# Graph attention and mixture of experts: groups 2 and 3 of the last stage treated as one unit

## The reference, cut to what matters

```python
def _gat_conv(x, W, att_src, att_dst, bias, src, dst):
    xw = (x @ W).reshape(N, H, CPH)
    e = leaky_relu(a_s[src] + a_d[dst], NEG)
    p = exp(e - segment_max(e, dst)[dst]);  alpha = p / segment_sum(p, dst)[dst]
    return segment_sum(xw[src] * alpha[:, :, None], dst).reshape(N, H * CPH) + bias
...
out = concatenate([h0, h1]) + x               # h0, h1: the two convolutions
x = x + layernorm(out) * gamma + beta
h = layernorm(x)                              # input of the experts
top_w, top_i = top_k(h @ Wg + bg, 2);  top_w = softmax(top_w)
out = x + sum over e of w_dense[:, e] * (gelu(h @ W1[e] + b1[e]) @ W2[e] + b2[e])
```

## Time and profile before

| | us |
|---|---|
| three runs, lowest, median, highest | 3035.05, 3036.59, 3038.42 |
| the profiled execution | 3036.07 |
| its span in the trace | 3034.2 |
| last stage, from the first `shares` to the first turned expert tile | 2007 to 2281 |
| busy in the whole span: PE, DVE, ACT, POOL | 2131.5, 2188.6, 1630.6, 1885.4 |

### The profile page before, as it was taken

One profiled execution on the slowest core, in us unless ns is written; L12 is line 12 of the kernel. 1 busy time (PEld: TensorE's weight loads), 2 busy tenths in 40 slices (PEclk: granted clock), 3 DMA queues, 4 the chain that ended last, 5 costly groups with the idle time before them and its releaser, 6 DMA issues.

```text
span 3034.2 us, 42972 instructions
## 1 busy us (share of the span) xinstructions
PE 2131.5 (70%) x11674; PEld 2015.1 (66%) x11675; DVE 2188.6 (72%) x4468; ACT 1630.6 (54%) x2613; POOL 1885.4 (62%) x1868
## 2 busy tenths in 40 slices
PE   4600002788887887888888888703449999999998
PEld 2400002787887787887878887603438999999997
DVE  7678877788887787888888887788864444444443
ACT  5424423687777776877777777624433333333332
POOL 5777767777777777777777777777771222222222
PEclk8855555898999898989998998855559999999999
DMA  9446993444444444444444444565772222222222
GB/s 357 135 145 179 159 239 123 127 127 143 147 128 127 140 150 127 127 152 139 128 127 147 143 127 127 167 218 168 260 257 37 38 37 37 38 38 37 38 37 31
DMA packets 278910, 395.04 MB, mean 130 GB/s; under 512 B 156236, under 2 KB 231569, under 8 KB 272257
## 3 DMA queue, kind: packets, MB, share of 16 engines
q1 hardware_dynamic: 202945, 244.92, 25.4%
q0 software_dynamic: 74000, 145.58, 20.9%
q10 hardware_dynamic: 1840, 3.06, 0.3%
HBM read 201.61 MB, written 191.79 MB: 130 GB/s over the span
## 4 chain that ended last, share of the span: by engine, by line
POOL 45%; PE 26%; issue 15%; DVE 7%; DMA 3%; ACT 2%; DVEq 2%; SPq 0%; POOLq 0%; ACTq 0%
POOL AR L935 43%; PE ps L1453 12%; PE ps L1459 12%; POOL placed L1003 1%; PE ps L1329 1%; DMA tables<-AR 1%; DVE group_stats L2020 1%; ACT AR L1262 1%; DVE AR L1718 1%; DVE AR L1765 1%; DMA state<-AR 1%; POOL AR L967 0%; DVEq L1760 0%; POOL room L974 0%; DVE AR L2144 0%
## 5 line engine op out<-in xcount | busy, mean ns | idle before, releaser
L935 POOL DMA_INDIRECT AR<-tables,idx x1391 | 1326.3, 954 | 425.6 <-issue 423.2
L1358 PE MATMUL ps<-table_parts,onehot 128*128 128x408 f32 (+1 forms) x5848 | 1202.1, 371 | 300.8 <-DVE AR L1845 161.2
L1358 PEld LDWEIGHTS ps<-table_parts,onehot 128*128 128x128 f32 x5848 | 1166.1, 209 | 336.9 <-DVE AR L1845 175.4
L1143 ACT COPY AR<-AR 128x1984 f32<-128x1984 f32 (+3 forms) x110 | 401.4, 3649 | 328.9 <-DVE AR L1765 286.2
L1012 POOL DMA_INDIRECT out<-AR,idb x105 | 184.0, 1753 | 568.5 <-issue 537.6
L1765 DVE TENSOR_TENSOR_SCAN AR<-ps,AR 128x512 f32<-128x512 f32 x404 | 454.2, 1196 | 0.0
L1453 PEld LDWEIGHTS ps<-AR 128*128 128x128 f32 x3360 | 393.0, 193 | 31.9 <-issue 26.6
L1453 PE MATMUL ps<-AR 128*128 128x128 f32 x3360 | 393.6, 276 | 26.5 <-DVE AR L2238 26.5
L1758 DVE TENSOR_TENSOR AR<-AR,ps 128x3968 f32<-128x3968 f32 (+1 forms) x51 | 356.6, 6991 | 0.0
L2238 DVE COPY AR<-AR 128x1024 f32 x210 | 151.1, 720 | 207.4 <-PE ps L1453 205.6
L1218 ACT ACTIVATE onehot<-onehot 128x1536 fp32r<-128x1536 f32 (+1 forms) x172 | 269.4, 1566 | 5.5
(11 more groups left out here) (345 smaller groups left out, 2456.7 us busy)
## 6 DMA issues: line engine op xcount, KB each, us to landing
state<-AR SPq DMA_DIRECT2D x50, 2232.0 KB
AR<-tables,idx POOLq DMA_INDIRECT x1440
AR<-in_L_ffn_W SPq DMA_DIRECT2D x16, 1024.0 KB
AR<-placed SPq DMA_DIRECT2D x420, 32.0 KB
AR<-adstart SPq DMA_DIRECT2D x50, 248.0 KB, 4.0
adstart<-room SPq DMA_DIRECT2D x21, 496.0 KB, 14.0
tables<-AR SPq DMA_DIRECT2D x49, 136.0 KB, 2.4
room<-tables SPq DMA_DIRECT2D x14, 476.0 KB, 4.2
```

What stands on the lines that cost most here:

```text
L935: pool.indirect_dma_start(out=G[s][:, j, 0:ROWT], out_offset=None, in_=table_rows, in_offset=bass.IndirectOffsetOnAxis(ap=idx[:, s, j:j + ...
L1143: return S.copy(to.rearrange("p j (h c) -> p j h c", h=HD)[:, :, :, a:z], of[:, :, 1:n + 1].rearrange("p (c h) j -> p j h c", h=HD)[:, :, ...
L1358: return T.matmul(bank[:, 0:z], mark, table_parts[:, k, v * w:v * w + z], start=(a == 0 and k == 0), stop=(a == LEV - 1 and k == PARTS - 1))
```

## The change

A unit is one group or a pair. In the first convolution the units are 0, 1, (2, 3), 4, 5, 6; in the second (0, 1), (2, 3), 4, (5, 6). The small operations of `shares`, of the new function `weights` (the five small ones taken out of `combine`), of the statistics, of `choose` and of `settle` are issued once a unit, over 14 tiles for a pair; the large operations stay one set a group. The statistics and `choose` still hold one instruction a tile where they had one a tile.

- On DVE a pair's `conclude(2)` is followed by `settle` of the unit before, then `conclude(3)`, then the second statistics of both groups. `shares(1, 3)` (groups 5 and 6 of the second convolution) stands behind these, and `weights` and both `combine` behind it.
- `share_of` has one buffer instead of two.
- On ACT the exponential for the next unit's shares stands ahead of the normalisation, no longer behind it.
- On POOL the gathers of groups 2 and 3 come ahead of the second convolution's rest of group 5; and a unit's places are issued together: 28 DMAs for groups 2 and 3. One group's gathers stand behind each of the first three units' places.
- On SP `own(7)` is issued ahead of the loop and the own rows are spread anew; the loop goes by units.
- On PE the ranks of a pair are one chain of 16 matmuls (before, 9 for a group).

```diff
+UNITS = ((0,), (1,), (2, 3), (4,), (5,), (6,))
+UNITS2 = ((0, 1), (2, 3), (4,), (5, 6))
+NU = len(UNITS)
+UT = 2 * GRP
+OWN_ORDER = ((1, 0), (1, 1), (1, 2), (1, 3), (1, 4), (0, 0), (0, 1), (0, 2), (0, 3), (1, 5), (1, 6), (0, 4), (0, 5), (0, 6))
...
             pool.wait_ge(fix_rows_stored, 48)
             for n in range(2):
                 last_states1(n)
-            last_states2(5, 2, GRP)
             for n in range(2, 4):
                 last_states1(n)
+            last_states2(5, 2, GRP)
             last_states2(6)
-            def place(n):
-
-                pool.wait_ge(places_ready, n + 1)
-                for k in range(2):
-                    for t in range(GRP):
-                        pool.indirect_dma_start(out=placed, out_offset=bass.IndirectOffsetOnAxis(ap=ipos[:, n % 2, k, t:t + 1], axis=0),
-                                                in_=pr[n % 4][:, t, :], in_offset=None).then_inc(tokens_placed[n % 4], 16)
-
-            for n in range(NG):
-                place(n)
-                if n + 4 < NG:
-                    last_states1(n + 4)
+            for u, unit in enumerate(UNITS):
+                pool.wait_ge(places_ready, u + 1)
+                for i, n in enumerate(unit):
+                    for k in range(2):
+                        for t in range(GRP):
+                            at = i * GRP + t
+                            pool.indirect_dma_start(out=placed, out_offset=bass.IndirectOffsetOnAxis(ap=ipos[:, u % 2, k, at:at + 1], axis=0),
+                                                    in_=pr[n % 4][:, t, :], in_offset=None).then_inc(tokens_placed[n % 4], 16)
+                if u < 3:
+                    last_states1(u + 4)
...
+                def store_rows(g):
                     sp.wait_ge(x_gnn_ready, g + 1)
...
+                for u, unit in enumerate(UNITS):
+                    for g in unit:
+                        rows_ahead(g)
+                    for g in unit:
+                        store_rows(g)
+                    if u == 2:
+                        for i in (12, 13):
+                            own(i)
+                    for e in ((), (), (1,), (2, 3), (4,), (5,))[u]:
+                        down_in(e)
...
+            for u, unit in enumerate(UNITS):
+                deviations(u, 0)
+                if u + 1 < NU:
+                    share_exps(0, u + 1)
+                act.wait_ge(group_scales_ready, 2 * u + 1)
+                for i, g in enumerate(unit):
+                    for t in range(GRP):
+                        at = i * GRP + t
+                        last = S.activation(halves[g][:, t, :], halves[g][:, t, :], ACT.Identity, bias=group_scale[:, 2, at:at + 1], scale=group_scale[:, 1, at:at + 1])
+                    last.then_inc(group_normalised, 1)
+                    if i == 0 and u >= 1:
+                        gate_exp(u - 1)
+                deviations(u, 1)
+                if u == 2:
+                    share_exps(1, 3)
+                act.wait_ge(group_scales_ready, 2 * u + 2)
+                for i, g in enumerate(unit):
+                    rows_normalised(g, i * GRP)
+            gate_exp(NU - 1)
...
+                dd()
+
+            def combine(k, g):
+
+                unit = [a for a in (UNITS, UNITS2)[k] if g in a][0]
+                at = unit.index(g) * GRP
+                z = share_of[:, k, :, at:at + GRP, :]
...
             shares(1, 0)
             run_maxima(2)
-            shares(1, 1)
+            weights(1, 0)
             combine(1, 0)
             run_sums(2)
+            combine(1, 1)
+            fix_maxima(2)
+            fix_sums(2)
+            shares(1, 1)
+            weights(1, 1)
+            combine(1, 2)
+            combine(1, 3)
             shares(1, 2)
-            fix_maxima(2)
-            combine(1, 1)
-            fix_sums(2)
-            shares(1, 3)
-            combine(1, 2)
-            shares(1, 4)
-            combine(1, 3)
+            weights(1, 2)
             combine(1, 4)
             shares(0, 0)
-            for g in range(NG):
-                combine(0, g)
+            for u, unit in enumerate(UNITS):
+                weights(0, u)
+                for g in unit:
+                    combine(0, g)
 
                 def next_shares():
-                    if g + 1 < NG:
-                        shares(0, g + 1)
-                    if 2 <= g <= 3:
-                        shares(1, 3 + g)
-
-                layer_stats(halves[g], g, 0, next_shares)
-                if g >= 1:
-                    choose(g - 1)
-                if 2 <= g <= 3:
-                    combine(1, 3 + g)
-                conclude(g)
+                        shares(0, u + 1)
+
+                layer_stats([halves[g] for g in unit], u, 0, next_shares)
+                if u >= 1:
+                    choose(u - 1)
+                conclude(unit[0])
+                if len(unit) == 2:
+                    settle(u - 1)
+                    conclude(unit[1])
+
+                def settle_or_shares2():
+                    if u == 2:
+                        shares(1, 3)
+                    elif u >= 1:
+                        settle(u - 1)
+
+                layer_stats([X[:, g * GRP:(g + 1) * GRP, :] for g in unit], u, 1, settle_or_shares2)
+                if u == 2:
+                    weights(1, 3)
+                    for g in UNITS2[3]:
+                        combine(1, g)
+            choose(NU - 1)
+            settle(NU - 1)
+
```

More of the change, by code:

```diff
@@ L1409, in _, with ranks, logits @@
             chain(2)
[L1411 to L1421, removed]
+            def ranks(u):
+                n = GRP * len(UNITS[u])
+                pe.wait_ge(masks_then_sum_ready, u + 1)
+                mk = route_of[:, 3, 0:n, :].rearrange("p t e -> p (t e)")
+                T.matmul(ps[7][:, 0:n * NEX], tri[:, :], mk, start=True, stop=False)
+                for d in range(1, n):
+                    T.matmul(ps[7][:, d * NEX:n * NEX], ones[:, :], mk[:, 0:(n - d) * NEX], start=False, stop=False)
+                T.matmul(ps[7][:, 0:n * NEX], ones[:, :], bc(mask_sum[:, u, :].unsqueeze(1), [P, n, NEX]), start=False, stop=False)
+                T.matmul(ps[7][:, 0:n * NEX], ones[0:1, :], bc(e8r[0:1, :].unsqueeze(1), [1, n, NEX]), start=False, stop=True).then_inc(ranks_then_totals_ready, 1)
+            def logits(g, first, t):
                 w = min(2, GRP - t)
@@ L1440, in _ @@
                     if t >= 2:
[L1441 to L1445, removed]
+                        logits(g, first, t - 2)
+                return logits(g, first, GRP - 1)
+            for u, unit in enumerate(UNITS):
+                if u >= 1:
+                    ranks(u - 1)
+                for i, g in enumerate(unit):
+                    mm = turn_rows(g, i * GRP)
+                mm.then_inc(logits_ready, 1)
+            ranks(NU - 1)
+            pe.wait_ge(masks_then_sum_ready, NU + 1)
+            T.matmul(ps[6][:, GRP * NEX:GRP * NEX + NEX], ones[:, :], mask_sum[:, NU, :], start=True, stop=True).then_inc(ranks_then_totals_ready, 1)
             def up(s, t):
@@ L2016, in _, with layer_stats @@
             spread_lasts(2)
-            def layer_stats(src_, g, q, meanwhile=None):
-                for t in range(GRP):
-                    V.bn_stats(group_stats[:, t, :], src_[:, t, :])
+            def layer_stats(rows, u, q, meanwhile):
+                n = GRP * len(UNITS[u])
+                for t in range(n):
+                    V.bn_stats(group_stats[:, t, :], rows[t // GRP][:, t % GRP, :])
                 dd()
-                for t in range(GRP):
+                for t in range(n):
@@ L2033, in shares @@
[L2033 to L2042, removed]
+                V.tensor_scalar(group_mv[:, 0:n, 1], group_mv[:, 0:n, 1], EPS, None, ALU.add).then_inc(variances_ready, 1)
@@ new lines, in layer_stats, with state_views @@
+                meanwhile()
+                dve.wait_ge(deviations_ready, NG + 2 * u + q + 1)
+                V.reciprocal(group_scale[:, 1, 0:n], group_scale[:, 0, 0:n])
+                dd()
+                V.scalar_tensor_tensor(group_scale[:, 2, 0:n], group_mv[:, 0:n, 0], -1.0, group_scale[:, 1, 0:n], ALU.mult, ALU.mult).then_inc(group_scales_ready, 1)
+            def state_views(k, unit):
+                where = (states1, states2)[k]
+                if len(unit) == 2 and (k == 0 or unit[0] == 0):
+                    a = unit[0] % 4
+                    flat = AR[:, states1_at + a * GRP * ROWS:states1_at + (a + 2) * GRP * ROWS] if k == 0 else eb2f[:, 0:2 * GRP * ROWS]
+                    return [(0, UT, flat.rearrange("p (t r) -> p t r", r=ROWS))]
+                return [(i * GRP, (i + 1) * GRP, where[g % 4]) for i, g in enumerate(unit)]
```

195 lines of the change are left out of this document (95 added, 100 removed).

## The result

The changed kernel takes 3074.44 us (median of four runs, 3072.96 to 3075.44) against 3035.82 for the kernel before on the same chip: ratio 1.0126, 95% interval 1.0111 to 1.0140, slower by 38.6 us. It was forecast at 3081, in a range of 3066 to 3096. One of the 27 runs of the kernel before beside experiments 1, 2, 3 and 5 had a granted clock of 0.742 where the others had 0.83 and took 3147.33 us; the ratios leave it out.

What follows compares the result with a forecast made beforehand. DVE and POOL were nearly full, the end set by DVE's trip through the last group. Alternating waits, savings included, put POOL's last places 45.2 us later: 3036.07 became 3081.3, so 3081, range 3066 to 3096.

Steps and rivals of the forecast that it cites:

- its chain: From POOL's first place on, six steps in which POOL and DVE wait in turn: last places 45.2 us later.
- the landing of a gather: On POOL's gathers of groups 4, 5 and 6: 5.54 us from the start of the last one to landing.
- POOL's time per DMA: In the last stage: 1.265 us a place with DVE at rest; 14 places 17.7, or 18.8 to 20.9 beside DVE.
- the case that every DMA costs 1.25 us: POOL's DMAs never slowed by DVE, as the skill infers: the sum would be 36 in place of 45 us.
- The savings: On DVE, small operations issued once for a pair, and waits for ACT that go: about 14 us less to do.
- The waits of 2.40 us: DVE's waits for ACT ahead of the second convolution's sum, at 2115.91 and a group later, would go.
- My term for that: ACT's exponential ahead of the normalisation: the normalisation ends 0.7 us later a trip (0 to 1.6), two trips counted.
- The fix row: POOL's write of it, 2.50 us late for DVE before, would come 2.2 us earlier (0 to 2.5).
- A: Rival: the same chain with POOL slowed throughout, +60 us, 3096; chance 0.09.
- B: Rival: only two of DVE's three waits for gathers open, the first being filled, +27 us, 3063; chance 0.06.
- C: Rival: gathers arrive in time and DVE's list, with fewer instructions, decides: -10 us, 3026; chance 0.04.
- D: Rival: the savings and the waits cancel, within 6 us; chance 0.03.

Runs made afterwards that it cites:

- experiment 1: The changed kernel with the gathers of groups 4, 5 and 6 each one batch earlier in POOL's list: 3035.65 us, 0.9982 of the kernel before.
- experiment 2: The changed kernel with only group 6's gathers moved ahead of the 28 places of groups 2 and 3: 3048.31 us, 1.0024 of the kernel before.
- (3): The changed kernel, DVE taking the next unit's shares behind second statistics and settling from the pair on, ACT's exponential likewise: 3050.24 us, 1.0031 of the kernel before.
- experiment 5: The changed kernel with single groups in the first convolution, pairs only in the second: 3036.49 us, 0.9987 of the kernel before.
- experiment 7: The kernel of experiment 6 with ACT's exponential for the next shares behind the normalisation again: 3031.62 us, 0.9969 of the kernel before.
- experiment 6: The changed kernel with single groups in the first convolution and the gathers one batch earlier: 3036.31 us, 0.9984 of the kernel before.

## Why the prediction was right

The mechanism was the one described, step for step. In the intervals of its chain:

| step | forecast, us | measured, us |
|---|---|---|
| 1. first place to group 4 landed | 32.7 | 30.3 |
| 2. DVE, to group 1's places | 11.4 | 11.7 |
| 3. to group 5 landed | 36.1 | 34.0 |
| 4. DVE, to the pair's places | 16.6 | 16.0 |
| 5. to group 6 landed | 49.9 | 46.6 |
| 6. to the last places | 57.9 | 58.5 |
| sum | 204.6 | 197.1 |

The kernel before needs 158.8 for the same stretch (2098.85 to 2257.68), so this is +38.3. Less 0.1 ahead of the first place and the 1.8 us by which this execution came to the stage earlier (2005.37 against 2007.17), and with 0.6 behind it, these are the 36.9 us between the two spans, 3071.1 and 3034.2.

**The term that was mis-sized: the landing of a gather.** I took 5.54 us from the start of the last gather for all three. It was 2.61 (2124.64 to 2127.25), 3.83 and 2.62: 7.6 us less in all, and the whole difference is 7.5. The other terms were off by 0.6 us a step at most and cancel: DVE's by +0.3, -0.6 and +0.6, POOL's from its first place to its last gather by +0.5, -0.4 and -0.4. The table of busy time shows why, by its DMA share (the last but one column), first of the kernel before in the stretch that the 5.54 comes from:

```profile
2192.00:2200.00 8.00, 7.44 (x37) 7.26 (x35) 6.73 (x20) 3.31 (x8) 6.48 (x6) 0.50 0.96 338
```

and of the changed kernel in the stretches of its three landings:

```profile
2122.00:2128.00 6.00, 0.00 (x0) 0.00 (x0) 0.61 (x4) 0.00 (x0) 2.84 (x3) 0.50 0.21 49
2167.00:2173.00 6.00, 2.41 (x13) 2.32 (x11) 4.10 (x17) 3.15 (x4) 2.42 (x3) 0.50 0.82 277
2230.00:2236.00 6.00, 0.00 (x0) 0.00 (x0) 0.39 (x2) 0.00 (x0) 2.94 (x4) 0.50 0.22 49
```

At a share of 0.21 and 0.22 the landing took 2.6 us, at 0.82 it took 3.8, at 0.96 it took 5.5. While DVE stands, little else is under way: SP's timeline has no DMA issued between 2108.59 and 2136.34 us, nor between 2190 and 2244.61, where the kernel before had stores and weights issued from 2183.24 to 2186. I had made this correction for POOL's own time per DMA and not for the transfer behind it. The experiments repeat it wherever a wait shows the landing: 2.55 (experiment 2) and 2.59 us (3) at shares of 0.26 and 0.22, 3.72 (2) and 3.72 (5) at 0.74 and 0.90, and 5.6 to 6.2 for group 0, at 1.00 to 1.03, in eight of the nine profiles. That the landing depends on the load is read from these, not from a run that changes the load alone.

**POOL's time per DMA** was right: 28 places took 36.5 us (2188.88 to 2225.37) against 36.9, and the first 14, beside two sums, 20.2 against 19.7. Of the DMAs that POOL issued while DVE stood for group 6, none took over 0.99 us; beside DVE's products and additions single ones took 1.7 to 2.3, as at 2138.93. The timelines of all nine profiles, from 2030 to 2275 us, say what goes with it: 256 of POOL's DMAs took over 1.3 us, and every one of them overlapped a large product or addition on DVE (128x896 or 128x1792); of the 921 that overlapped none, the longest took 1.09. That is what ran beside, in kernels that were not built to separate it. The Trainium skill (SBUF — State Buffer, section "Who interferes with whom") infers that additions and products of two SBUF inputs leave the making of descriptors alone. These traces speak against that.

The prediction gave 36 us for the case that every DMA costs 1.25 us; its own bounds make that 37.6, or 3073.7, and the measured time lies nearer to it than to the forecast. That is chance. The 14 places beside DVE took 20.2 and 21.6 us and not 17.7; it was the landings that took the 7.6 us off.

**The savings** that the trace shows alone were right within 0.3 us in two cases: the pair's choice 4.89 us (2174.12 to 2179.01) against 5.15, the weights of a pair 2.16 (to 2099.24) against 2.15. The waits of 2.40 us are gone (0.37 is left of them). In all DVE is busy for 7.1 us less from the first `shares` to the last place, where the terms without the two waits come to about 9. In experiment 5 these savings, left to themselves, are worth 4.0 us, where DVE was to have 14 less to do: the pair (2, 3) is not in it, and the earlier exponential took some back. My term for that was 0.7 us on two trips. For group 0 it was 0.6, as the waits for ACT show, first of the changed kernel and then of the kernel before:

```profile
2064.01 2.04 DVE L2200 TENSOR_TENSOR AR<-AR,gam 128x1792 f32<-128x1792 f32 x1 [4.23 <-ACT AR L1312]
```

```profile
2066.50 2.03 DVE L2141 TENSOR_TENSOR AR<-AR,gam 128x1792 f32<-128x1792 f32 x1 [3.61 <-ACT AR L1262]
```

For group 1 it was 0.35. But it is paid on later trips too: experiment 7 gives 4.2 us for all of them. How much of it the changed kernel pays behind its long waits was not tried apart.

**The fix row** was written 1.2 us earlier in the stage (23.0 us from its start and not 24.2), not 2.2, and the first place started 0.1 us earlier and not 0.65.

**The rivals.** A (POOL slowed throughout, 3096) fell with the 28 places. B (only two waits open, 3063) did not happen; the time lies between it and the forecast for another reason, the short landings. The second wait was short, 1.7 us, but the first was 12.9. C (DVE's fewer instructions decide, 3026) is what experiments 1 and 5 come near when the circle is open: 4 to 5 us under the kernel before, not 10. D (within 6 us) is 33 us away.

## What to carry to other kernels

When two engines work through lists written by hand, look at each wait for what stands behind it on the waiting engine: if the other engine's list needs that before it reaches the work waited for, they alternate, and both lists' times add up. Here that cost 38 us. Making a batch larger on one of them (28 writes in place of 14) moves everything behind it in that list, so a load that stands behind the batch has to be moved ahead of it. And a latency read where the transfer engines are full is too long for a stretch in which they will be idle.

## What the runs showed that I had not expected

- The landing of seven gathers of 128 rows took 2.6 us from the start of the last at a DMA share of 0.2, and 5.5 at 0.96.
- POOL's indirect DMAs took over 1.3 us only beside DVE's large products and additions: 256 of the 499 that overlapped one, and none of the other 921.
- ACT's exponential with its 1.28 us table load, put ahead of a normalisation that DVE waits for, cost 4.2 us in a stage of 261 (experiment 7), though each trip's wait shows only 0.5 to 0.6.
- The pair in the first convolution gained nothing even with its gathers in time: 261.3 us of stage with it (experiment 1) and 261.1 without (experiment 6). POOL waits 13.29 us for the pair's places and then issues to the end without another wait; that this takes back what the pair saves DVE is read from the timeline, and no run tried it apart.
